# A graph network's edge loop: which engine fetches the source rows of three of a turn's 112 edge tiles, and in which order the first steps run

## What is computed

```python
z = jnp.concatenate([x[dst], x[src], edge_attr], axis=-1)
msg = jax.nn.sigmoid(z @ Wf + bf) * jax.nn.softplus(z @ Ws + bs)
summed = jax.ops.segment_sum(msg, dst, num_segments=n)
out = summed / jnp.maximum(cnt, 1.0)[:, None]      # cnt: edges of a node
out = (out - rmean) * jax.lax.rsqrt(rvar + BN_EPS) * gamma + beta
return out + x
```

## Time and profile before

| | |
|---|---|
| median of 3 runs | 2086.69 us (2085.7 to 2089.22) |
| the profiled execution's own time | 2085.8 us |
| its span, first to last instruction | 2084.0 us |
| granted TensorE clock, mean share of full | 0.94 |
| busy: PE, DVE, ACT, POOL | 1540.8, 1745.7, 1618.0, 1481.8 us |
| layer 1, layer 2, finish | to about 1010, to about 2040, to 2084 us |

### The profile page before, as it was taken

How to read it: one execution, slowest core, us unless ns; L and a number is a source line. 1 busy time by engine, 2 the same in 40 slices (tenths; PEclk the granted TensorE clock), 3 DMA queues, 4 the chain that set the end, 5 groups by cost and what they waited for, 6 DMA issues and landing times. The chain is left out here.

```text
span 2084.0 us, 41078 instructions
## 1 busy us (share of the span) xinstructions
PE 1540.8 (74%) x8321; PEld 1266.5 (61%) x8321; DVE 1745.7 (84%) x3574; ACT 1618.0 (78%) x3692; POOL 1481.8 (71%) x1575
## 2 busy tenths in 40 slices
PE   7777777777677777777587777777777777777773
PEld 6666666656556666565466566566665555666652
DVE  6799988989889889798638999798788887988887
ACT  5699887878778778688457889698787777877884
POOL 6577777777777777777267777777777777777770
PEclk9999999999999999999799999899899999999995
DMA  8455555555555555555475555555555555555552
GB/s 293 119 169 161 169 171 158 159 161 168 161 159 158 170 159 158 161 166 162 134 230 152 171 167 170 151 168 164 156 168 161 165 161 158 161 161 167 159 148 62
DMA packets 168890, 339.48 MB, mean 163 GB/s; under 512 B 62702, under 2 KB 93030, under 8 KB 168643
## 3 DMA queue, kind: packets, MB, share of 16 engines
q0 software_dynamic: 73824, 200.29, 32.4%
q1 hardware_dynamic: 93298, 135.27, 21.7%
q10 hardware_dynamic: 1522, 1.72, 0.3%
HBM read 315.49 MB, written 19.81 MB: 161 GB/s over the span
## 5 line engine op out<-in xcount | busy, mean ns | idle before, releaser
L402 POOL DMA_INDIRECT pre<-s_rows,ends x1498 | 1417.8, 946 | 482.9 <-issue 445.8
L516 PE MATMUL pre_ps<-rhs,lhs 128*128 128x256 f32 x3136 | 832.7, 409 | 450.5 <-DVE lhs L774 449.8
L516 PEld LDWEIGHTS pre_ps<-rhs,lhs 128*128 128x128 f32 x3136 | 592.6, 199 | 667.6 <-DVE lhs L774 418.8
L798 DVE TENSOR_TENSOR pre<-pre_ps,pre 128x1024 f32<-128x1024 f32 x378 | 460.6, 1219 | 50.5 <-DMA pre<-s_rows,ends 50.5
L609 ACT ACTIVATE logs<-pre 128x512 f32<-128x512 f32 x392 | 246.9, 630 | 306.6 <-DVE pre L798 265.9
L774 DVE SCALAR_TENSOR_TENSOR lhs<-lhs,base_f,sum_ps 64x256 f32<-64x256 int32 x784 | 373.3, 476 | 114.7 <-issue 51.8
L531 PEld LDWEIGHTS sum_ps<-hot,msg 128*128 128x128 f32 x3136 | 435.1, 201 | 55.9 <-issue 25.0
L531 PE MATMUL sum_ps<-hot,msg 128*128 128x64 f32 x3136 | 414.3, 278 | 29.6 <-DVE sums L817 19.4
L603 ACT COPY rhs<-dst_ps 64x256 f32<-64x256 f32 x792 | 290.0, 366 | 62.6 <-issue 31.3
L809 DVE TENSOR_TENSOR msg<-soft_ps,logs 128x512 f32<-128x512 f32 x392 | 271.0, 691 | 13.3
L802 DVE SCALAR_TENSOR_TENSOR soft_ps<-soft_ps,pre 128x512 f32<-128x512 f32 x392 | 270.4, 690 | 1.1 <-ACT soft_ps L616 1.0
(11 more groups left out here) (92 smaller groups left out, 573.7 us busy)
## 6 DMA issues: line engine op xcount, KB each, us to landing
lhs<-dge_and_destination_cols SPq DMA_DIRECT2D x196, 512.0 KB
single<-s_rows SPq DMA_DIRECT2D x1792, 1.0 KB
pre<-s_rows,ends POOLq DMA_INDIRECT x1498, 2.8
s_rows<-logs SPq DMA_DIRECT2D x8, 512.0 KB, 7.3
s_rows<-x_t SPq DMA_DIRECT2D x7, 512.0 KB, 12.0
s_rows<-msg SPq DMA_DIRECT2D x6, 512.0 KB, 7.0
x_rows<-pre SPq DMA_DIRECT2D x12, 256.0 KB
out<-y_out SPq DMA_DIRECT2D x12, 256.0 KB, 2.3
```

Source lines behind the costliest of these rows:

```text
L402: nc.gpsimd.indirect_dma_start(pre[:, slot(k, j), i, 0:width], None, rows, bass.IndirectOffsetOnAxis(ap=ends[:, k, j * TILES + i, 0:1], ax ...
L516: ins = nc.tensor.matmul(pre_ps[:, j % 2, i, :], lhs[:, j // 2, edges], rhs[:, j, i // 2, :], start=True, stop=not plain(b, k, j))
L798: nc.vector.tensor_tensor(rows, pre_ps[:, j % 2], rows, ALU.add).then_inc(s_pre[j], 1)
```

## The change

**Tiles.** Three tiles a turn are no longer gathered by POOL: the last tiles of steps (3, 3), (6, 2) and (6, 3). The first two are short: the host's layout leaves their last 25 of 128 edges empty, 103 rows are loaded (350 of the 352 padding edges are moved there), and the rest of `single` is cleared once. POOL issues 109 gathers a turn.

**SP** loads the rows of the first short tile in halves 0 to 6 (13, 17, 13, 17, 13, 17, 13 rows) and those of the second in halves 7 to 13 (17, 15, 17, 15, 17, 15, 7), issues three lists and two block numbers a turn (with the first ones ahead of the first turn), and three placements: the first short tile's in half 7, the second's in half 13, behind its last rows, and ACT's tile in half 0 of the next turn. Its wait for all stores of the table moves from half 2 to half 0.

**ACT** loads the 128 rows of (6, 3): in steps 2 to 23 of a turn it reads six numbers into registers and issues one row's DMA behind each activation, two behind the last.

**First steps.** The staging buffers are used in another order, with `hot` first; ACT's wait for `flagged` comes ten copies later; POOL clears `sums[:, 1]` in layer 1 in place of DVE; DVE makes the one-hot of steps 1 to 3 early in the step; PE's `turn` of a plain step is written behind the product before. The group table has five or six more empty rows on either side.

```diff
-SINGLE = (BODY - 1, SLOTS - 1, TILES - 1)
-SINGLE_ROWS = 12
+SINGLES = ((3, 3), (6, 2), (6, 3))
+ACT_FROM, ACT_ROWS = 2, 6
+SINGLE_ROWS = 103
+CUT = ((0, 13, 30, 43, 60, 73, 90, 103), (0, 17, 32, 49, 64, 81, 96, 103))
...
+            def place_act(b):
+                k, j = SINGLES[2]
+                sp.wait_ge(act_rows_in, b * (16 * P))
+                sp.sem_inc(passed, 1)
+                sp.wait_ge(s_soft[(j - RING) % SLOTS], b * BODY + (k - BODY))
+                sp.sem_inc(passed, 1)
+                sp.dma_start(pre[:, slot(k, j), TILES - 1, :], single[:, 2, :]).then_inc(act_single_in, 16)
+
+            def load_singles(i, part):
+                rows = range(CUT[i][part], CUT[i][part + 1])
...
+            def place_singles(i, b):
+                k, j = SINGLES[i]
+                sp.wait_ge(singles_in, b * (32 * SINGLE_ROWS) + (i + 1) * (16 * SINGLE_ROWS))
+                sp.sem_inc(passed, 1)
+                done(sp, s_soft, group_no(b, k), j, RING)
+                sp.sem_inc(passed, 1)
+                sp.dma_start(pre[:, slot(k, j), TILES - 1, :], single[:, i, :]).then_inc(single_in, 16)
+
+            def singles(b, half):
                 if half == 0:
...
+                    if not isinstance(b, int):
+                        place_act(b)
+                    sp.wait_ge(list_in, b * 64 + 48)
                     sp.sem_inc(passed, 1)
+                    load_list(2, act_list_in)
                     if isinstance(b, int):
                         for r in range(len(s_stage)):
...
+                            sp.wait_ge(s_out[r], stores_of(r))
                     else:
...
+                        sp.wait_ge(single_in, b * 32)
                         sp.sem_inc(passed, 1)
...
+                if half == BODY:
+                    sp.wait_ge(list_in, b * 64 + 64)
+                    sp.sem_inc(passed, 1)
+                    place_singles(0, b)
+                load_singles(half // BODY, half % BODY)
+                if half == 3:
+                    load_list(1, list_in)
+                if half == BODY + 2:
+                    load_block(0, group_no(b, SINGLES[0][0]) + BODY)
+                if half == BODY + 4:
+                    sp.wait_ge(list_in, b * 64 + 80)
+                    sp.sem_inc(passed, 1)
+                    load_list(0, list_in)
+                if half == BODY + 5:
+                    load_block(1, group_no(b, SINGLES[1][0]) + BODY)
                 if half == 2 * BODY - 1:
...
+                    sp.wait_ge(single_in, b * 32 + 16)
+                    sp.sem_inc(passed, 1)
+                    place_singles(1, b)
...
-                    gather(s_dram, F2, k, j, TILES - ((k, j) == SINGLE[0:2]))
+                    gather(s_dram, F2, k, j, TILES - ((k, j) in SINGLES))
...
+            def load_row(row):
+                if row:
+                    act.dma_start(single[row[0]:row[0] + 1, 2, :], s_dram[bass.ds(row[1], 1), :]
+                                  ).then_inc(act_rows_in, 16)
...
-            def exponents(g, j, at):
+            def exponents(g, j, at, at_rows):
                 done(act, s_pre, g, j, 0)
                 done(act, s_msg, g, j, 2)
                 nc.scalar.activation(logs[:, j % 2, :, 0:F], pre[:, at, :, 0:F], ACT.Exp, scale=-1.0)
+                load_row(next(at_rows))
                 nc.scalar.activation(logs[:, j % 2, :, F:F2], pre[:, at, :, F:F2], ACT.Exp).then_inc(s_expo[j], 1)
...
+                load_row(next(at_rows))
...
-                if live(0) and four_back:
+                if live(0) and (four_back or SLOTS * k + j):
                     one_hot(g, k, j)
...
-                if first and isinstance(b, int) and step < 4:
-                    nc.vector.memset(t["sums"][:, 1, step * (NPAD // 4):(step + 1) * (NPAD // 4)], 0.0).then_inc(zeroed, 1)
```

More of the change, by code:

```diff
@@ new lines, in place_act @@
+            def place_act(b):
[7 more added lines that the diff above has]
+                rows = range(CUT[i][part], CUT[i][part + 1])
+                at_row = nc.values_load_multi_w_load_instructions(
+                    sp_src[:, i, rows[0]:rows[-1] + 1], engines=[ENG.SP], min_val=0, max_val=NPAD - 1,
+                    skip_runtime_bounds_check_because="sources are rows of the table")[1]
+                for p, r in zip(rows, at_row):
+                    sp.dma_start(single[p:p + 1, i, :], s_dram[bass.ds(r, 1), :]).then_inc(singles_in, 16)
@@ L326, in load_singles @@
[L326 to L338, removed]
@@ L541, in one @@
                 for j in range(SLOTS):
-                    if plain(b, k, j):
-                        turn(SLOTS * k + j)
-                    else:
+                    if not plain(b, k, j):
                         product(b, k, j)
@@ L604, in rows, with row_numbers @@
                 ins.then_inc(s_rows[j], 1)
-            def exponents(g, j, at):
+            def row_numbers(b, step):
+                first_row = (step - ACT_FROM) * ACT_ROWS
+                n = max(min(ACT_ROWS, P - first_row), 0) if first_row >= 0 else 0
+                if first_row == 0:
+                    act.wait_ge(act_list_in, b * 16 + 16)
+                    act.sem_inc(passed, 1)
+                    if isinstance(b, int):
+                        for r in range(len(s_stage)):
+                            act.wait_ge(s_out[r], stores_of(r))
+                    else:
+                        act.wait_ge(act_single_in, b * 16)
+                        act.sem_inc(passed, 1)
+                regs = nc.values_load_multi_w_load_instructions(
+                    sp_src[:, 2, first_row:first_row + n], engines=[ENG.Activation], min_val=0, max_val=NPAD - 1,
+                    skip_runtime_bounds_check_because="sources are rows of the table")[1] if n else ()
+                return iter([(first_row + i, r) for i, r in enumerate(regs)] + [None] * (ACT_ROWS - n))
+            def load_row(row):
[3 more added lines that the diff above has]
+            def exponents(g, j, at, at_rows):
                 done(act, s_pre, g, j, 0)
@@ L642, in one @@
                     window_cols(g, j, cols_at)
[L643 to L645 removed]
+                    at_rows = row_numbers(b, SLOTS * k + j)
+                    exponents(g, j, slot(k, j), at_rows)
+                    logarithms(g, j, at_rows)
+                    gate(g, j, at_rows)
                     step = SLOTS * k + j - 3
[L647 to L649 removed]
+                    if first and isinstance(b, int) and step in range(0, 4 * len(in_x1), 4):
+                        act.wait_ge(s_out[5 + step // 4], stores_of(5 + step // 4))
                     if first and isinstance(b, int) and 0 <= step < DOUBLES:
@@ L667, in _ @@
             if first:
-                n = [0, 0]
+                n = [0]
                 def after(ins):
```

170 lines of the change are left out of this document (90 added, 80 removed).

## The result

| | before | after |
|---|---|---|
| median | 2086.3 us, 4 runs (2085.7 to 2089.22) | 2461.3 us, 4 runs (2459.6 to 2461.59) |
| the profiled execution's own time | 2085.8 us | 2459.6 us |
| its span | 2084.0 us | 2457.7 us |
| granted TensorE clock | 0.94 | 0.86 |
| a turn of SP in the middle of layer 1 | 138.7 us | 164.1 us |

What follows compares the result with a forecast made beforehand. POOL's gathers were taken to bound the kernel (138.8 us a turn), with SP to become the limit at 146.5; 2085.8 + 67 (layer 1) + 63 (layer 2) = 2216 us, range 2160 to 2300.

Steps and rivals of the forecast that it cites:

- SP paces at its own cost: SP's queue, not POOL, sets the turn: 146.5 us, against POOL's new 136.3; chance 0.70.
- 206 rows still 0.41 apart: Sign in SP's queue: rows issue every 0.41 us as before; 206 instead of 128 add 32.0 us a turn.
- ACT's rows: Row issues and reads on ACT, costed at nothing: at most 16.5 us a turn stick out, under its 23.1 of waiting.
- The late first `lhs`: In the first turn the `lhs` load for steps 4 and 5 moves from 48.86 to about 68 us.
- the tail of layer 1: From layer 1's last `lhs` load to its last `sums`: 13.5 us instead of 22.5, 9 less.
- Twelve numbers take 947 ns, eight 718: 57 ns for one number and 263 for the read: Price of SP's register reads; 14 reads of 206 numbers instead of 11 of 128 add 5.2 us a turn.
- The landing waits: SP waits for its rows to land before placing tiles, halves 13 and 7: 1.9 and 1.2 us a turn.
- The first steps: New order of the first steps, costed at nothing; up to 6 us gained if SP had room.
- POOL still sets the pace: Rival: SP's turn stays under 136.3 us, so fewer gathers make the kernel faster, 2048 us; chance 0.10.
- No difference: Rival: SP's turn is 138 to 139 us with landing waits nothing and lists half price, 2082 to 2090; chance 0.04.
- ACT sets the pace: Rival: ACT's issues are not hidden by the activation before, so its turn is 180 us, 2630 in all; chance 0.04.
- The two queues hinder each other: Rival: ACT's issues slow SP's rows by 0.07 us each where they meet, 5.2 a turn, 2285 in all; chance 0.12.

Runs made afterwards that it cites:

- even cuts: The changed kernel with only SP's cuts moved, so that its register reads start at multiples of four numbers: 2211.7 us, 1.0591 of the kernel before the change.
- the first set: First runs of four follow-up kernels, all run again later; the kernel before the change itself took 2861 us in it instead of 2087.
- the last kernel: SP loads only (6, 2)'s short tile, twelve rows a half from half 2; ACT loads (6, 3) in reads of twelve: 2067.6 us, 0.9901 of the kernel before the change.
- the kernel before it: One short tile on SP, 103 rows in halves 2 to 6, ACT reading twelve numbers every second step: 2163.6 us, 1.0361 of the kernel before the change.

## Why the prediction was right, and where it was wrong

**What held.** SP paces at its own cost (the case with 0.70): its waits for PE went from 38.6 us a turn to none, POOL got long gaps, and L838 waits for the `lhs` DMA. "206 rows still 0.41 apart" held: the median spacing is 0.412 us. ACT's rows cost next to nothing: one issue is 0.21 us in the median and lies beside the running activation, as its timeline shows for the first of a step (ACT is the engine, ACTq its queue).

```profile
723.05 0.62 ACT L671 ACTIVATE logs<-pre 128x512 f32<-128x512 f32 x1
723.06 0.47 ACTq L665 DMA_DIRECT2D single<-s_rows  x1
723.58 0.62 ACT L673 ACTIVATE logs<-pre 128x512 f32<-128x512 f32 x1
```

The late first `lhs` held as well: forecast at about 68, it came at 70.0. The load of half 4 came at 93.38 instead of 89, and the tail of layer 1, from the last `lhs` load (1178.89) to the last `sums` (1192.60), took 13.7 us, where 13.5 had been worked out. In between lie 1085.5 us, against 969 in the forecast; both layers are longer by the same cause.

**The step that failed** is one term: "Twelve numbers take 947 ns, eight 718: 57 ns for one number and 263 for the read", and with it "14 reads of 206 numbers instead of 11 of 128 [...] +5.2". The change added some 24 us there, not 5.2. SP's turn was 164.1 instead of 146.5, and 17.6 x 13.3 turns = 234 us; 2216 + 234 = 2450, of a measured 2459.6. With reads near the price of the sum, 16.7 us a turn where it had 15.4, the sum comes out: 2211.7 was measured for even cuts, 2216 forecast. The fit went through two sizes that are both multiples of four and that both start at multiples of four, so its slope, 57 ns, is that of a group of four divided by four. The new cuts have 13, 15 and 17 numbers and start anywhere; the fit was carried over to reads of another kind without a bound of its own. The Trainium skill ("Runtime: NRT & Kernel Launch", section "Instruction fetch mechanics") puts a register load (TENSOR_LOAD) at about 200 ns a register, even in bulk; it speaks of loads from HBM, where these read a list in SBUF. The reads that don't start at a multiple of four agree with it, 0.20 us a number; the others don't, at about a quarter of that, and for them the measurement decides. An estimate with that page's figure as the upper end of the read price, 206 x 0.2 + 14 x 0.27 = 45 us a turn against 15.4, would have put the end of the range at 2216 + 29.6 x 13.3, near 2610, and 2461 inside.

**Terms that were off by little.** The landing waits were 1.5 to 2.2 us a turn, not 3.1 (both ends had been kept for them). The first steps, costed at nothing, are worth 2.2 us where SP has room, not 6; what they are worth in the changed kernel no run tells apart.

**The rivals.** *POOL still sets the pace* is refuted by SP's missing waits; it needed a turn of SP under 136.3, and with even starts it is 146.2. *No difference* needed 138 to 139, and falls with it. *ACT sets the pace* would have needed gaps between its activations; there are 7.3 us of them in all ahead of L673, and ACT waits 40.9 us a turn for DVE. *The two queues hinder each other* is the one to be careful with, since a slower kernel than forecast seems to speak for it. Rows with and without ACT's queue cost the same within 1.1 us a turn, where this rival had 5.2, and the dear reads come without ACT. What had spoken for it was a single issue of 0.41 us at the start. An effect of ACT's first row can be seen on ACT itself: behind the first activation its issue takes 0.45 to 0.5 us instead of 0.21, which is hidden.

**Open** are the 10 us between 2450 and the measured time, the reads that stay off the rule (the 1.00 and 1.90 us of the two first ones, the two levels on ACT), the stall of 2.0 to 2.4 us in the kernel without ACT's tile, and what disturbed the first set. In the last kernel the spread of the rows, SP's tile and ACT's reads were changed together, so the 96 us to the kernel before it are put down to the spread by the `lhs` spacing and not by a run that changes it alone.

## What to carry to other kernels

An engine that only issues is a resource like the others: add up its work against the pace of the loop, and for each stretch that feeds the next steps, not for the turn as a whole (20 and more rows in each of five halves took 96 us more than 12 in each of eight and 7 in a ninth, with the same reads on ACT but another tile). Let every register read of a list start at a multiple of four numbers, and take whole groups of four where that is free. When a price is fitted from rows, look at whether the new instances differ from the fitted ones in something other than size (here the start); if they do, the fit is one bound and needs another.

## What the runs showed of the hardware

- Register reads cost by where their first number stands. From a multiple of four 12 numbers took 0.95 us and 16 1.17, from other starts 13 took 2.87 and 17 3.67; on ACT six numbers took 0.76 to 0.94 or 1.51.
- A 1 KB row with a register address costs SP 0.41 us, of which 0.228 is the issue; on ACT the issue is 0.21 and lies beside the activation.
- SP's rows are not slowed by 128 issues of ACT a turn (a turn's 206 rows take 86.0 to 86.9 us without and 86.2 to 87.1 with them; an issue has a median of 228 ns whether or not one of ACT overlaps it).
- Behind the branch that ends a loop turn SP's next instruction starts 2.4 to 3.3 us later, in the changed kernel and with even cuts, though nothing that the profile shows is waited for.
- PE's granted clock, a mean between its levels of 1.2 and 2.4 GHz, was 0.86 instead of 0.94 in the kernel in which PE stands still more (69% busy instead of 74%), and its busy time rose by 165 us. It doesn't set this time: in its loop turns SP never waits for PE.
